# The order of steps in a two-lane fused block kernel: a table of turns, and a merge by weights

## What is computed

```python
x = x + 0.5 * ffn(layernorm(x))        # attention (16 heads of 8), then a mixture of 4 experts
x = x + mamba(layernorm(x))            # projection, convolution, SSM over time, gated norm, MLP
x = x + 0.5 * ffn(layernorm(x))        # the same weights as the first

def ffn(x):
    x = x + attn(layernorm(x, ln1))    # depthwise conv of 3 taps, qkv, rotary, causal softmax, projection
    h = layernorm(x, ln2)
    e = argmax(h @ router)             # one of 4 experts for each token
    return x + where_e(silu(h @ gate[e]) * (h @ value[e]) @ down[e])
```

## Time and profile before

| | |
|---|---|
| Median of 3 runs | 2296.11 us |
| Profiled execution, first to last instruction | 2293.9 us |
| TensorE matmul busy | 1976.4 us, 86% |
| VectorE busy | 1528.3 us, 67% |
| ScalarE busy | 1054.4 us, 46% |
| GpSimd busy | 280.5 us, 12% |
| Mean granted TensorE clock | 0.932 |
| DMA | 11.25 MB, 5 GB/s |

### The profile page before, as it was taken

How to read it: one execution, slowest core, us unless ns; L and a number is a source line. 1 busy time by engine, 2 the same in 40 slices (tenths; PEclk the granted TensorE clock), 3 DMA queues, 4 the chain that set the end, 5 groups by cost and what they waited for, 6 DMA issues and landing times. The chain is left out here.

```text
span 2293.9 us, 35596 instructions
## 1 busy us (share of the span) xinstructions
PE 1976.4 (86%) x11712; PEld 1038.1 (45%) x11824; DVE 1528.3 (67%) x3811; ACT 1054.4 (46%) x1650; POOL 280.5 (12%) x305
## 2 busy tenths in 40 slices
PE   4788898897969899889796988898879789989978
PEld 2344444453434444444443444454444445444443
DVE  6477487584848758667584876857757585784844
ACT  3534535453543544545353453554535355445451
POOL 1011202101001220210101021021010103112100
PEclk8988998998989999999898999999989899999998
DMA  2000000000000000000000000000000000000000
GB/s 91 1 1 6 1 5 1 1 1 6 1 7 1 6 1 5 2 1 1 5 1 7 5 2 1 6 1 1 2 5 2 5 1 1 1 1 1 1 6 5
DMA packets 11935, 11.25 MB, mean 5 GB/s; under 512 B 864, under 2 KB 10464, under 8 KB 11744
## 3 DMA queue, kind: packets, MB, share of 16 engines
q1 hardware_dynamic: 11744, 8.84, 1.3%
HBM read 6.74 MB, written 2.10 MB: 4 GB/s over the span
## 5 line engine op out<-in xcount | busy, mean ns | idle before, releaser
L560 PE MATMUL wring<-scratch,wv 128*128 128x512 f32 x1024 | 548.6, 644 | 21.9 <-DVE scratch L1101 19.0
L1037 DVE TENSOR_REDUCE mx<-aring 128x1 f32<-128x512 f32 (+3 forms) x704 | 429.4, 638 | 203.7 <-PE aring L494 200.2
L748 ACT ACTIVATE prob_mem<-aring 128x512 f32<-128x512 f32 x640 | 363.2, 597 | 274.5 <-PE aring L509 272.1
L774 ACT ACTIVATE scratch<-wring 128x512 f32<-128x512 f32 x256 | 152.6, 596 | 517.8 <-PE wring L560 516.3
L507 PE MATMUL aring<-stq,stkT 128*128 128x384 bf16 (+3 forms) x975 | 251.5, 312 | 66.2 <-DVE mx L1037 35.3
L492 PE MATMUL aring<-stkT,stq 128*128 128x384 bf16 (+3 forms) x961 | 251.0, 306 | 33.6 <-DVE mx L1037 24.7
L560 PEld LDWEIGHTS wring<-scratch,wv 128*128 128x128 f32 x1024 | 188.0, 204 | 187.2 <-issue 122.3
L535 PE MATMUL acc<-scratch,ep 128*128 128x512 f32 x512 | 262.8, 595 | 0.5 <-DVE scratch L1115 0.5
L698 ACT ACTIVATE stq<-aring 64x1024 bf16<-64x1024 bf16 x192 | 195.2, 1017 | 92.0 <-PE aring L419 90.5
L509 PE MATMUL aring<-neg_queries,identb 128*128 128x128 bf16 x1024 | 192.9, 225 | 23.3 <-ACT stq L698 19.7
L1109 DVE SCALAR_TENSOR_TENSOR scratch<-scratch,wring 128x512 f32<-128x512 f32 x256 | 174.4, 681 | 52.8 <-ACT scratch L774 51.5
(11 more groups left out here) (206 smaller groups left out, 2592.1 us busy)
## 6 DMA issues: line engine op xcount, KB each, us to landing
x<-in_x SPq DMA_DIRECT2D x8, 256.0 KB, 2.8
wv<-in_wv SPq DMA_DIRECT2D x1, 2048.0 KB, 10.7
out_x<-x SPq DMA_DIRECT2D x8, 256.0 KB, 2.2
w<-in_w SPq DMA_DIRECT2D x2, 256.0 KB, 4.8
W_in<-in_W_in SPq DMA_DIRECT2D x1, 322.0 KB, 12.1
attn_w<-in_attn_w SPq DMA_DIRECT2D x1, 192.0 KB, 2.8
W_out<-in_W_out SPq DMA_DIRECT2D x1, 128.0 KB, 3.9
ident<-in_consts SPq DMA_DIRECT2D x1, 64.0 KB, 1.9
```

The lines of the kernel that those rows point to most:

```text
L560: last = pe.matmul(ring[:], wv[:, e, o:o + P], hm[e % 2][:], start=True, stop=True)
L748: act.activation(probs[x % EXPS], ring[:], ACT.Exp, scale=float(HD) ** -0.5).then_inc(a_freed[t % SLOTS], 1)
L1037: dve.tensor_reduce(dst, src_ap, AX_X, ALU.max).then_inc(a_freed[t % SLOTS], 1)
```

## The change

`TURNS` goes. In its place stand a weight for each kind of step and a function that merges two lists of weights phase by phase. In each phase the lane comes next that would be the less far along, in parts of its own total, at the middle of its next step. So both lanes begin and end each phase together. The steps, what each issues, and the dependencies stay as they are.

```diff
-TURNS = (
-    "0010010010011002001010120123301203011104431000022b4600030030320140133330203310511211100100"
...
-)
+A_SHARE = {"stats": 3, "norm": 2, "hT": 3, "qkv": 2, "high": 1, "mid": 2, "low": 3, "qkT": 1, "max": 0.9, "shift": 1.5, "exp": 0.9,
+           "pv_last": 2, "back": 1.5, "yT": 1.5, "proj": 1.5, "e_stats": 3, "e_norm": 2, "e_hT": 1.5, "logits": 2}
+E_SHARE = {"mask": 1.2, "gate": 1.2, "value": 2, "last_down": 1, "back": 2}
+M_SHARE = {"stats": 3, "norm": 2, "uT": 1.5, "xbc": 1.5, "dt": 1, "conv": 2.3, "z": 1.5, "step_size": 4, "BC": 2.5, "sums": 1,
...
+def merged(phases):
+    order = []
+    for first, second in phases:
+        at, done = [0, 0], [0.0, 0.0]
+        shares = (first, second)
+        total = [sum(x) or 1.0 for x in shares]
+        while at[0] < len(first) or at[1] < len(second):
+            left = [k for k in range(2) if at[k] < len(shares[k])]
+            k = min(left, key=lambda k: (done[k] + shares[k][at[k]] / 2) / total[k])
+            done[k] += shares[k][at[k]]
+            at[k] += 1
+            order.append(k)
+    return order
...
-        order = [k for turn in TURNS for k in [0] * int(turn, 36) + [1]] + [0] * (4 * a)
+        sa = [A_SHARE[step[0]] for _, step in A_TASKS]
+        se = [E_SHARE[step[0]] for _, step in E_TASKS]
+        sm = [M_SHARE[step[0]] for _, step in M_TASKS]
+        order = merged([(sa, se + sm), (sa, se + sm), (sa, se), ([] if last else sa, se)])
```

More of the change, by code:

```diff
@@ L129 @@
 E2_AT = [2 * NE + 2 * NM, 3 * NE + 2 * NM]
-TURNS = (
-    "0010010010011002001010120123301203011104431000022b4600030030320140133330203310511211100100"
-    "100100110011010101201232112111111044301000220a50212203133102031325120332311121110010010010"
-    "111010101100311333342113e3ogm100010010111010101012120330322303i3ni"
-)
+A_SHARE = {"stats": 3, "norm": 2, "hT": 3, "qkv": 2, "high": 1, "mid": 2, "low": 3, "qkT": 1, "max": 0.9, "shift": 1.5, "exp": 0.9,
+           "pv_last": 2, "back": 1.5, "yT": 1.5, "proj": 1.5, "e_stats": 3, "e_norm": 2, "e_hT": 1.5, "logits": 2}
+E_SHARE = {"mask": 1.2, "gate": 1.2, "value": 2, "last_down": 1, "back": 2}
+M_SHARE = {"stats": 3, "norm": 2, "uT": 1.5, "xbc": 1.5, "dt": 1, "conv": 2.3, "z": 1.5, "step_size": 4, "BC": 2.5, "sums": 1,
+           "xs": 1, "xsT": 1, "BT": 1, "G": 1, "decay": 1.5, "state": 1, "head_decay": 1.5, "Y0": 1, "Y1": 4, "sumsq": 2,
+           "out": 2.5, "mh_var": 1, "mh_norm": 2.5, "hT": 1.5, "up": 2, "last_down": 1.5, "back": 2}
+def merged(phases):
[11 more added lines that the diff above has]
+    return order
 def alone(stage):
```

## The result

The changed kernel takes **2617.58 us** (median of four runs, 2605.81 to 2618.43), the kernel before, on the same chip, 2295.52. The ratio is 1.139, with a 95% interval from 1.137 to 1.142. The direction was forecast, the size was not: 322 us lost where 62 were expected, well above the range (2296 to 2420).

What follows compares the result with a forecast made beforehand. TensorE, busy 86% of 2293.9 us, was taken as the bound, its idle time as the question. Phases 3 and 4 at +49 and phases 1 and 2 at +13 made +62: 2355.9, plus 2.2, so 2358 us; range 2296 to 2420.

Steps and rivals of the forecast that it cites:

- (a): Attention's head in phases 3 and 4 loses expert filler: about 34 us with TensorE busy some 20, saving 5.1 us.
- (b): Attention's middle in phases 3 and 4 gets 20 more large matmuls: 79.6 us against 68.5, plus 11.1.
- the densest stretch of before: 481 to 511 us of the earlier trace, TensorE busy 29.1 of 30 us; its share was assumed for the new middle.
- (c): Attention's tail in phases 3 and 4 gets expert steps: between a gain of 0.8 and a loss of 2.8, taken as plus 1 us.
- The clock, set at nothing: Phases 3 and 4: a nearly empty head lowers TensorE's clock, a filled tail avoids that; the two were set against each other.
- (d): Phases 1 and 2, with mamba: -4 + 8.2 - 2.6 = +1.6 us each, times 8 = +13; bounds -9 and +8.
- nearly even: Phases 1 and 2: work moved out of the head and mamba's stretch nearly balances, +1.6 us a phase.
- The faster case: Rival, chance 0.10: even turns close mamba's idle TensorE time, 71 us back against 49 lost, 2274 us.
- No difference: Rival, chance 0.07: semaphores and three banks a lane let engines slip past the order; time stays 2296 us.
- the small loss: Rival, chance 0.13: middle without gaps, head 31.5 us; about +1 a phase in 3 and 4, 2310 us.
- The large loss: Rival, chance 0.15: in-order engines stop both lanes; +12 us in each of seven phases, +5 in eight, 2420 us.

## Why the prediction was right in its sign and wrong in its size

**(a) The head: right.** Forecast were 34 us with TensorE busy some 20; measured are 35.5 with 21.2. The chain needs its time with or without filler. What was missed is its clock, 0.71 where the full head had 0.92.

**(b) The middle: the share was the failed step.** The content was right: forecast 77.3 us, measured 76.6 busy. But I let it run at the 97% of the densest stretch of before, on the ground that an expert step after every three or four of attention resembles that stretch. It took 86.4 us, a share of 89% and just above the upper bound of 85.7, "no gap of before filled". The whole middle of before, which stood in the earlier trace rows, had a share of 88%. The idle time of the middle was 8.4 us before and is 9.8 now. The gaps lie behind each shift, where two copies of a microsecond stand between neighbouring attention steps, and an even merge puts its steps where the gaps are not. Steps placed on purpose in them gave 82 us back over the whole program, and with full heads 108 of the 124 of phases 3 and 4. So the mechanism named was right, and its middle value should have been the upper bound, +17.2: measured is +17.9, forecast was +11.1.

**(c) The tail: right in size**, +1.7 us against +1 (14.2 in place of 12.5).

**The clock, set at nothing: wrong.** The head's loss and the tail's gain did not even out: the third phase went from 0.91 to 0.89 and its TensorE busy time from 104.4 to 107.5 us; the fourth from 0.92 to 0.88 and from 101.6 to 110.3. The rule of the Trainium skill quoted in the prediction (TensorE: Matmul & The Clock Gate, "What's actually happening"), that activity lifts the throttled state, agrees with the runs: every kernel with filler matmuls had the higher clock (0.942 for 0.882, 0.914 for 0.882, 0.956 and 0.953 for 0.932). Only the inference fell that the new tail would save what the new head loses.

Phases 3 and 4 thus cost 15.9 and 20.1 us each, 126 in all, where 49 were forecast and 125 was the upper bound. Why the fourth costs 4 us more than the third was not looked into.

**(d) Phases 1 and 2: the failed term, and the largest.** Forecast were +1.6 us each with +8 as the upper bound, measured are +24.5. Two steps of it failed.

The head did not shrink to 37. The first maximum comes 43.6 us after the pick in phase 2 and came after 42.6, though nine large matmuls left it (26 in place of 35 by the lists, not 24 in place of 33). So the 4 us were not saved, and TensorE's idle time in the head rose to 8 us from 2.1. This is the same fact that (a) had used in phase 3, that the chain sets the head's length, and I didn't apply it here, because TensorE was 96% busy in that head and seemed the bound.

And "nearly even" was wrong for mamba. The matmuls and attention steps that move forward do cost their time where they now stand: mamba's stage begins 15 us later (its statistics at 75.7 us of phase 2 in place of 60.3). The upper bound held the nine matmuls and not the attention steps, because these were to be saved later. They were not. From mamba's first step to the pick, phase 2 of the kernel before, of the changed one, and of the one with mamba merged and one exchange:

```profile
341.70:440.70 99.00, 85.99 (x587) 46.55 (x592) 59.37 (x166) 54.08 (x96) 21.02 (x17) 0.93 0.01 4
...
381.10:489.90 108.80, 88.24 (x523) 47.30 (x522) 53.15 (x153) 47.09 (x85) 21.44 (x17) 0.84 0.01 1
...
352.40:461.30 108.90, 89.56 (x591) 47.16 (x590) 59.88 (x166) 52.87 (x95) 21.34 (x17) 0.90 0.01 3
```

The changed kernel has eighteen attention steps fewer there than the table and sixteen fewer than the third kernel. It takes 9.8 us longer than the first and as long as the third. So the even merge makes mamba's stretch some 109 us long, whether 69 or 85 attention steps stand in it: its waits set its length, and taking attention out saved nothing. TensorE is idle for 20.6 us in place of 13.0, at a clock of 0.84 for 0.93. The prediction did name the test, "above 168, mamba's chain was starved and (d) is wrong". The time is what came (184.3 and 186.5). But sixteen more attention steps beside it made mamba's merged stretch neither shorter nor longer, so it is where they stand that counts, not how many there are.

**The rivals.** The faster case fell: phases 1 and 2 got longer. No difference and the small loss fell with them. The large loss, order against order, came nearest, but not in price: its 12 us and 5 us a phase measured 18 and 24.5. It was given a chance of 0.15. The Trainium skill's advice (Perfetto Trace Analysis, "Optimization Strategy") to interleave regimes is borne out only with a place: spread evenly it cost 14%, put into heads and copy gaps it gave 186 us back.

**What stays open.** In phases 3 and 4 the cause is shown by giving it back (108 of 124 us). In phases 1 and 2 the loss has a place, but two thirds of it were never given back in the changed kernel, and no run says which waits of mamba's merged stretch make it 10 us longer. Mamba's merge with the one exchange still costs 88 us, 11 a phase; its convolutions are a part (the third one comes at 84.7 us of phase 2 in place of 78.0). How the 322 us divide between idle time and clock can't be said by cause, only by account (180 and 143), for the one mostly comes with the other. And phases that have the same order of steps differ: the table's third phase measured 117.6 to 121.9 us in different kernels, the merged phase 2 with full heads 174.1 to 183.4 in one and the same. So differences of a few microseconds a phase, such as the 20 us of the merged expert stretch (2.5 a phase), can't be given to the order alone.

## What to carry to other kernels

An even merge balances totals, but a gap is at a place: where one lane must wait for a copy, the other lane needs a step just there whose input is already made, and in one order here two neighbouring turns the wrong way round cost 66 us. When costing a new order, first list the gaps of the old one with what stands in each, and ask of the new order what stands there; take "no gap filled" as the middle value unless a row names the filler. A stretch whose length is set by a chain doesn't get shorter when its filler leaves, even if the engine looks 96% busy in it, but the filler takes its time where it goes.

## What the runs showed of the hardware

Behind a 4.08 us gap of TensorE the clock was granted at 0.55 for the next 12 us, and the sixteen small matmuls of the norm's sum took 3.57 us; with the two turns exchanged they took 1.95 at a clock of 1.00. Two phases with the same order of steps in one kernel took 175.2 and 183.3 us, the longer one with less idle time and a clock of 0.86 for 0.94.

Matmuls whose result is thrown away can pay: 160 of them (20 in each of eight attention stages), put where TensorE idled in the kernel before, made it 1.1% faster (2295.3 to 2268.9) and lifted the mean clock from 0.932 to 0.953. With 68 in each of sixteen stages, full heads included, the same kernel lost 127 us at a clock of 0.956. In the changed kernel, spread over all its idle places, they lifted the clock by 0.06 and saved next to nothing (3 us).
